# Normalising two steps ahead, high parts before signs, and TensorE's program written out, in a two-layer convolution kernel

## The reference

```python
# layer 0
x = x + _L0_conv_ref(_gn(x), dw, pw, att, gatt)   # depthwise 3x3, then three 64x64 channel mixes
# layer 1
x = x + _L1_conv_ref(_gn(x), w)                   # conv3x3(sign(.), sign(w)) * mean|w| of each output channel

def _gn(v, G=32, eps=1e-5):                       # over pairs of channels of one image
    m = jnp.mean(g, axis=(2, 3, 4), keepdims=True)
    s = jnp.var(g, axis=(2, 3, 4), keepdims=True)
    return ((g - m) / jnp.sqrt(s + eps)).reshape(v.shape)
```

## Time and profile before

| | before |
|---|---|
| median of 3 runs | 1948.15 us (1945.4 to 1950.78) |
| profiled execution, its own time | 1947.49 us |
| its span | 1945.5 us |
| TensorE busy | 93% |
| VectorE busy | 86% |
| ScalarE busy | 66% |
| GpSimd busy | 28% |
| DMA | 138 GB/s of HBM traffic over the span |
| TensorE's clock, mean of the span | 0.994 of full speed |

### The profile page before, as it was taken

How to read it: one execution, slowest core, us unless ns; L and a number is a source line. 1 busy time by engine, 2 the same in 40 slices (tenths; PEclk the granted TensorE clock), 3 DMA queues, 4 the chain that set the end, 5 groups by cost and what they waited for, 6 DMA issues and landing times.

```text
span 1945.5 us, 81090 instructions
## 1 busy us (share of the span) xinstructions
PE 1807.5 (93%) x35562; PEld 1531.9 (79%) x35562; DVE 1667.6 (86%) x2578; ACT 1275.6 (66%) x1367; POOL 535.5 (28%) x285
## 2 busy tenths in 40 slices
PE   0099999999999999999999999999999999999997
PEld 0077777988876776899978787799997777799996
DVE  5568889888898889888898888988889888988887
ACT  2066776777666776677766677677766677677774
POOL 0032222223222222222222232223323222232221
PEclk9999999999999999999999999999999999999999
DMA  9925555555655565556555556556655565433223
GB/s 205 220 68 152 151 151 133 152 157 152 151 126 153 151 151 142 142 152 151 151 131 153 141 151 151 132 150 155 152 151 136 151 151 151 106 78 76 76 76 99
DMA packets 279270, 271.50 MB, mean 140 GB/s; under 512 B 16576, under 2 KB 278848, under 8 KB 279104
## 3 DMA queue, kind: packets, MB, share of 16 engines
q1 hardware_dynamic: 279104, 269.23, 55.1%
HBM read 134.95 MB, written 134.22 MB: 138 GB/s over the span
## 4 chain that ended last, share of the span: by engine, by line
PE 82%; DVE 9%; SPq 3%; issue 3%; ACT 2%; DMA 1%; DVEq 0%; ACTq 0%
PE psA L484 71%; PE psB L484 11%; SPq L249 3%; DVE ring L850 1%; DVE bnt L685 1%; ACT xh L365 1%; DVE ring L876 1%; DVE aggr L791 1%; DVE xc L842 1%; DVE sums L697 1%; DVE psL L878 1%; DMA ring<-in_x 1%; ACT xn L361 1%; DVE ring L882 1%; SPq L256 0%
## 5 line engine op out<-in xcount | busy, mean ns | idle before, releaser
L484 PE MATMUL psA<-xh,W 64*64 64x512 f16 (+1 forms) x19456 | 1670.5, 361 | 37.3 <-ACT xh L365 30.8
L484 PEld LDWEIGHTS psA<-xh,W 64*64 64x64 f16 x19456 | 1176.2, 106 | 194.7 <-issue 50.7
L484 PE MATMUL psA<-xl,W 64*64 64x512 f16 (+1 forms) x9984 | 1144.8, 361 | 0.3 <-issue 0.3
L301 POOL TENSOR_TENSOR xl<-xc,xn 128x1024 f16<-128x1024 f32 (+2 forms) x264 | 532.6, 2019 | 1331.4 <-ACT xn L361 1331.4
L484 PEld LDWEIGHTS psA<-xl,W 64*64 64x64 f16 x9984 | 635.0, 106 | 81.9 <-issue 1.5
L484 PE MATMUL psB<-pk,W 64*64 64x512 f16 (+3 forms) x5568 | 638.0, 341 | 3.4 <-DVE pk L861 2.3
L384 ACT ACTIVATE sg<-ring,columns 128x1024 f16<-128x1024 f32 (+2 forms) x270 | 297.3, 1106 | 510.8 <-DVE ring L850 494.4
L365 ACT ACTIVATE xh<-xc 64x1024 f16<-64x1024 f32 (+1 forms) x528 | 543.1, 1031 | 9.5
L850 DVE SCALAR_TENSOR_TENSOR ring<-psA,columns,ring 128x1024 f32<-128x1024 f32 x256 | 328.5, 1283 | 213.0 <-PE psA L484 213.0
L484 PEld LDWEIGHTS psB<-pk,W 64*64 64x64 f16 x5568 | 340.9, 106 | 29.1 <-issue 9.1
L685 DVE BATCH_NORM_STATS2 bnt<-ring 128x6 f32<-128x512 f32 x512 | 326.5, 680 | 0.1
(11 more groups left out here) (90 smaller groups left out, 139.1 us busy)
## 6 DMA issues: line engine op xcount, KB each, us to landing
out_y<-ring SPq DMA_DIRECT2D x512, 256.0 KB, 3.2
ring<-in_x SPq DMA_DIRECT2D x448, 256.0 KB, 4.0
ring<-in_x SPq DMA_DIRECT2D x32, 512.0 KB, 13.9
pk<-in_w1T SPq DMA_DIRECT2D x2, 144.0 KB, 8.0
ring<-in_w1n SPq DMA_DIRECT2D x2, 144.0 KB, 7.9
grp<-in_same_group SPq DMA_DIRECT2D x1, 64.0 KB, 6.2
ring<-in_dw SPq DMA_DIRECT2D x2, 2.2 KB, 5.8
ring<-in_att SPq DMA_DIRECT2D x1, 16.0 KB, 2.0
```

Source lines behind the costliest of these rows:

```text
L301: ins = nc.gpsimd.tensor_tensor(xl[:, slot:slot + rows, 1:W + 1], xc[:, j:j + rows], xn[:, k:k + rows, 1:W + 1], ALU.subtract)
L484: mm = pe.matmul(bank[out0:out0 + C, c0:c1], weights[src0:src0 + C, :], src[src0:src0 + C, slot:slot + rows, width[0]:width[0] + width[1]] ...
```

## The change

Four edits:

- VectorE normalises chunk t+2 at the end of step t, after everything else, instead of chunk t+1 behind `add_layer0`. Two chunks are normalised before the first step.
- ScalarE's step begins with the high parts of chunk t+1, and the signs come second.
- `add_layer1` is two functions: `add_left` (L880, L884) stays where it was, and `add_right` (L889), which now counts `y_rdy`, comes after `take_part`. In `take_part` the column sums come after `bn_stats`. The small operations of the statistics come after `pack`, ahead of `normalise`.
- TensorE's program has no loop: all 256 steps are written out.

```diff
@@ ScalarE
             for t in range(ALL):
+                if t + 1 < ALL:
+                    high_of(t + 1)
                 if t + 1 >= LAG:
                     signs_of(t + 1 - LAG)
-                if t + 1 < ALL:
-                    high_of(t + 1)
@@ TensorE
-                with pe.Fori(first, NC // 4 - 1) as v:
-                    for q in range(4):
-                        step_one(img, Chunk(v, q), img, Chunk(v, q - LAG))
+                for i in range(4 * first, NC - 4):
+                    step(img, i)
@@ VectorE
             def take_part(g):
                 img, i = divmod(g, NC)
                 dve.wait_ge(ld[g % 2], 32 * ld_count(g))
-                take_borders(img, i)
                 at = place(img, i)
-                bn_tuples(ring[:, at:at + CE], i).then_inc(bn_done, 1)
+                bn_tuples(ring[:, at:at + CE], i)
+                take_borders(img, i).then_inc(bn_done, 1)
...
+            def add_left(img, ch):
+                n = img * NC + ch.i
+                here, right, left = halves(img, ch)
                 if n > 0:
                     dve.wait_ge(y_rdy, n)
                 dve.wait_ge(rnd_rdy, n + 1)
...
+            def add_right(img, ch):
+                here, right, left = halves(img, ch)
+                nc.vector.scalar_tensor_tensor(out=here[:, :, HW:W], in0=right, scalar=wmean[:, 0:1],
+                                               in1=here[:, :, HW:W], op0=ALU.mult,
                                                op1=ALU.add).then_inc(y_rdy, 1)
...
             normalise(*of(0))
+            normalise(*of(1))
             for t in range(ALL):
                 img, a = divmod(t, NC)
                 if t > 0:
                     add_layer0(*of(t - 1))
-                if t + 1 < ALL:
-                    normalise(*of(t + 1))
                 if t > LAG:
-                    add_layer1(*of(t - LAG - 1))
+                    add_left(*of(t - LAG - 1))
                 for g in parts_at(t):
                     if g < ALL:
                         take_part(g)
+                if t > LAG:
+                    add_right(*of(t - LAG - 1))
+                if a == 0:
+                    mean_of_x1(img)
+                if t + 1 >= LAG:
+                    pack(*of(t + 1 - LAG))
                 if img + 1 < NB:
                     if a == AGGR_STEP:
                         stats_parts(img + 1)
...
-                if a == 0:
-                    mean_of_x1(img)
-                if t + 1 >= LAG:
-                    pack(*of(t + 1 - LAG))
+                if t + 2 < ALL:
+                    normalise(*of(t + 2))
```

More of the change, by code:

```diff
@@ L696, in take_borders @@
                         nc.vector.reduce_sum(sums[p0:p1, img % 2, 1:2], ring[p0:p1, lo:lo + W], AX.X)
-                        nc.vector.tensor_copy(sums[p0:p1, img % 2, 4:6], ring[p0:p1, lo:lo + W:W - 1])
+                        ins = nc.vector.tensor_copy(sums[p0:p1, img % 2, 4:6], ring[p0:p1, lo:lo + W:W - 1])
+                return ins
             def stats_piece(p):
@@ L702, in stats_piece @@
                 for i in range(lo, hi):
-                    take_borders(0, i)
                     at = place(0, i)
-                    ins = bn_tuples(ring[:, at:at + CE], i)
+                    bn_tuples(ring[:, at:at + CE], i)
+                    ins = take_borders(0, i)
                 return ins
@@ L864, in pack, with halves @@
                 ins.then_inc(pk_rdy, 1)
-            def add_layer1(img, ch):
-                n = img * NC + ch.i
+            def halves(img, ch):
                 at = place(img, ch.i)
                 here = ring[:, at:at + CE].rearrange("p (s w) -> p s w", s=G)
+                return (here, rnd[:].bitcast(I16)[:, :, 0:2 * HW:2],
+                        psL[:, ch.par, 0:G * HW].rearrange("p (s w) -> p s w", s=G))
+            def add_left(img, ch):
+                n = img * NC + ch.i
+                here, right, left = halves(img, ch)
                 if n > 0:
@@ L872, in add_layer1 @@
                 dve.wait_ge(rnd_rdy, n + 1)
[L874 to L878, removed]
+                nc.vector.scalar_tensor_tensor(out=left, in0=right, scalar=-PACK,
                                                in1=psB[:, ch.par, 0:G * HW].rearrange("p (s w) -> p s w", s=G),
@@ L882, in add_layer1 @@
                 nc.vector.scalar_tensor_tensor(out=here[:, :, 0:HW], in0=left, scalar=wmean[:, 0:1],
-                                               in1=here[:, :, 0:HW], op0=ALU.mult,
+                                               in1=here[:, :, 0:HW], op0=ALU.mult, op1=ALU.add)
+            def add_right(img, ch):
+                here, right, left = halves(img, ch)
+                nc.vector.scalar_tensor_tensor(out=here[:, :, HW:W], in0=right, scalar=wmean[:, 0:1],
+                                               in1=here[:, :, HW:W], op0=ALU.mult,
                                                op1=ALU.add).then_inc(y_rdy, 1)
@@ L915, in _ @@
                         scale_of_group(img + 1)
[L916 to L919 removed]
+                if t + 2 < ALL:
+                    normalise(*of(t + 2))
             add_layer0(*of(ALL - 1))
[L921 removed]
+            add_left(*of(ALL - LAG - 1))
+            add_right(*of(ALL - LAG - 1))
             for g in range(ALL + 1 - LAG, ALL):
@@ L924, in _ @@
             for g in range(ALL - LAG, ALL):
-                add_layer1(*of(g))
+                add_left(*of(g))
+                add_right(*of(g))
 def kernel(x, L0_conv_depthwise_weights, L0_conv_pointwise_weights, L0_conv_attention_weights,
```

3 lines of the change are left out of this document (1 added, 2 removed).

## The result

| | before | changed |
|---|---|---|
| median | 1946.42 us of 20 runs (1942.06 to 1951.83) | 1954.41 us of 20 runs (1945.83 to 1966.08) |
| ratio | | 1.0046, interval 1.0031 to 1.0062 |
| profiled execution | 1947.49 us, span 1945.5 | 1962.04 us, span 1959.9 |
| TensorE's clock, mean | 0.994 | 0.999 |

The changed kernel is slower by 0.5%, 8 us. Its times spread over 20 us, twice those of before.

What follows compares the result with a forecast made beforehand. The prediction took TensorE to bound the ordinary step of 6.94 us. Image ends -33, old stalls -8.8, new-code stalls +53 and overlap -2 gave +9 us, hence 1957 us; its own range was 1945 to 1968.

Steps and rivals of the forecast that it cites:

- xh waits: TensorE waiting for ScalarE's xh, placed at image ends: 30.8 us in 21 waits, forecast to fall by 25 us.
- Image ends: Normalising two steps ahead and high parts first let VectorE and ScalarE keep up at the ends of images: -33 us.
- half-speed stretches: TensorE at half clock after four of the seven image ends, 1.7 us each; all four forecast to go, 7 us.
- The stalls of new code: TensorE written out waits for instruction fetch about every nine steps: 24 groups at 2.2 us, 53 us for 8.8.
- the later stores: Chunks complete later, so stores and loads go 0.6 us later; a reason for taking 2.2 us a stall group.
- A mechanism of queues: About 280 instruction packets, negligible in volume, each wait in the DMA queues behind loads and stores.
- Registers and branches worth nothing: Removing TensorE's loop registers and branches saves 0 to 0.01 us a step.
- The split of the layer-1 addition and the order of the statistics: On VectorE, work is moved and none added; stores go 0.6 us later, price by itself nothing.
- (a): Rival: fetch stalls only at the rate of all seven stretches, 30 us; 1936 us, faster; chance 0.25.
- (b): Rival: stalls belong to the entry of a loop, so all eight vanish when written out; 1906 us; chance 0.11.
- (c): Rival: loads fall behind later stores, VectorE waits, steps take 7.2 us; 1992 us; chance 0.18, shared with (d).
- (d): Rival: half-speed stretches follow fetch stalls, five at 1.7 us adding 8 us; chance 0.18, shared with (c).

Runs made afterwards that it cites:

- e1: The changed kernel with TensorE's loops put back, keeping the new order on VectorE and ScalarE: 1911.85 us, ratio 0.9827.
- e5: The changed kernel, written out, with the right half of the layer-1 addition directly behind the left: 1962.88 us, ratio 1.008.
- e4: e1 with two more passes of each loop written out in images 1 to 7, eight more steps of new code each: 1933.22 us, ratio 0.9937.
- e3: The changed kernel with each load from chunk 41 on bringing one of four rows: 1905.52 us in one run; with stores cut likewise, 1909.43 us.
- e10: The changed kernel with whole loads and stores that write one of four rows: 1914.42 us in one run.
- e7: e1 with a loop body of 8 steps passed three times in images 1 to 7, instead of 4 steps passed six times: 2024.94 us, ratio 1.042.
- e6: e1 with ScalarE's signs again ahead of the high parts: 2033.11 us, ratio 1.0467.
- e2: The kernel before with TensorE's loops written out and nothing else changed: 1983.96 us, ratio 1.0205.

## Why the prediction was right or wrong

It said 1957 us and slower; 1954.41 was measured, in the forecast's own range. On its profiled execution the sum was +9 us, and the span grew by 14.4: 45.1 more of stalls, 21.4 less of xh waits, 6.8 less at half speed and 1.9 less of waits for the statistics' matrix product make +15. That the number came within 3 us is in part luck, as the changed kernel's executions spread over 20 us; that the sum came within 6 on the profiled one is not, but it has offsetting errors in it.

- *Image ends, -33 us.* Right in size: the order alone gives -33 (e1) or -30 (without loops). Of its parts, the xh waits fell by 21.4 us, not 25: I had divided 30.8 by seven ends, though one wait of 8.7 of it stands at the start of the kernel (the longest) and no order of steps touches it. What remains at the ends is 0.6 us, not the 5.6 I had left. These two errors, 8.7 and 5.0 us, went against each other. The four half-speed stretches went, as I had let them (7 us), and the wait for the matrix product of the statistics (1.9, where I had 1). The terms make 30 us.
- *The stalls of new code, +53 us in place of 8.8.* Right: 53.2 us in 54 pieces in place of 8.1, in groups nearly nine steps apart, and 284 packets for about 280. They are 23 groups of 2.3 us for my 24 of 2.2. Two reasons beside it were wrong. That there are none without loads: five, some 4 us, stand in the last image. And the later stores, for which I had in part taken 2.2 and not 1.26 us a group, play no part (e5). What speaks for 2.2 is e4: with eight more steps of new code, images 1 and 3 do stall in them, image 5 still doesn't. So two of the three stretches without a stall had been cut off in time, as I had said.
- *A mechanism of queues.* Right in kind: the packets cost next to nothing by their number and nearly all by the traffic beside them (e3, e10), and each stall ends behind the landing of a packet that had started late. What holds its start back isn't shown; I had put it to waiting behind loads and stores.
- *Registers and branches worth nothing.* It holds for a body that is kept. Against what I wrote of the branch, a fetch is forced where the target isn't held: e7 shows it at each of 14.
- *The split of the layer-1 addition and the order of the statistics "move VectorE's work and add none".* Wrong by 72 us of busy time: what an operation takes depended on whether GpSimd's xl ran beside it. It did not show in the time, because VectorE waits for TensorE in an ordinary step of both kernels. It decides as soon as it meets the wrong operation (e6).
- *The rivals.* (a) fell with the result, 53.2 us of stalls and not 30, and with e4; (b) fell with e2. (c) happened in traces only: stores land in 3.9 us and the steps stay at 6.94, but its sign, a wait of VectorE for ring loads, is there 7 times, 2.5 us in all.
- (d) *Half speed after fetch stalls*: none behind the 51 of the changed kernel, the longest 2.04 us. But it does happen: once in e1 (behind 2.05 us), twice in e4 (2.08 and 2.56), each worth up to 1.7 us, and not behind one of 2.17 us in e2. That it came to nothing here is luck.

## What to carry to other kernels

Judge writing out a loop by the traffic beside it: this engine's new code was all but free at two thirds of the bytes and cost 2% at all of them, and on the page only "issue" and the packets of the instruction queue show it. A loop body short enough to be kept (four steps here) costs nothing and saves the fetch; one twice as long was worse than no loop, 2025 us against 1954. Take a change of order and a change of code size apart before keeping either: here the one was worth -33 us and the other +42, and together they looked like a change that does nothing.

## What the hardware showed that I had not expected

- A VectorE operation with two inputs in SBUF that meets GpSimd's xl ends some 0.54 us behind it: 0.75 us became 2.26, 0.70 became 0.88. One with an input from PSUM, L882, kept its 0.75 us. A copy of two numbers a partition ended with xl: its mean is 978 ns with 13 such meetings in 16, and 255 with one.
- A loop body of some 1110 TensorE instructions runs again without a fetch; one of some 2220 is fetched in each pass, and each of 14 branches back cost 2.3 to 4.5 us, 3.5 on average.
- In the changed kernel TensorE began no block of 16 KB of new code sooner than 1.22 us after the landing of a packet, and at its 51 "issue" waits 1.25 to 1.58 us after it.
- Cutting the loads to a quarter, with all of the code still new, left 0.3 of 45.8 us of issue waits; cutting the stores left 4.9.
